# One DVE instruction of 2048 elements for two neighbouring products of a CIN kernel

## What is computed

```
e = stack(tbl_f[ids[:, f]] for f in 0..38)             # 1024 x 39 x 16, float32
xk = e
for W, b in three layers:                              # W is 39 x fields(xk) x 128
    z  = einsum('bhd,bkd,hks->bsd', e, xk, W) + b
    z  = relu(z)
    xk, direct = z[:, :64], z[:, 64:]                  # last layer: all 128 are direct
z = sum over d of the direct parts                     # 1024 x 256
y = relu(relu([z, dense_ctx] @ W_top1 + b1) @ W_top2 + b2) @ W_top3
```

## Time and profile before

| | |
|---|---|
| median of 3 runs | 1320.3 us (1320.02 to 1326.73) |
| the profiled execution | 1325.62 us, span 1323.8 us |
| granted TensorE clock, mean | 0.996 |
| instructions on DVE | 965 |
| busy share of the span | PE 94%, DVE 82%, POOL 69%, ACT 50% |
| the chain that ended last, by engine | PE 76%, POOL 10%, issue 7%, DVE 6%, ACT 1% |

### The profile page before, as it was taken

How to read it: one execution, slowest core, us unless ns; L and a number is a source line. 1 busy time by engine, 2 the same in 40 slices (tenths; PEclk the granted TensorE clock), 3 DMA queues, 4 the chain that set the end, 5 groups by cost and what they waited for, 6 DMA issues and landing times.

```text
span 1323.8 us, 15099 instructions
## 1 busy us (share of the span) xinstructions
PE 1247.7 (94%) x4078; PEld 768.8 (58%) x4078; DVE 1090.1 (82%) x965; ACT 663.1 (50%) x704; POOL 910.8 (69%) x581
## 2 busy tenths in 40 slices
PE   0289999999999999999999999999999999999989
PEld 0136666666656666666655666666666666666633
DVE  1149888989999888988998888989999888989850
ACT  1124555545554555556554555555554555555532
POOL 6668778876888678876886678886888655555520
PEclk9999999999999999999999999999999999999999
DMA  6198777787887777887897677878887777777500
GB/s 184 27 217 206 178 192 183 201 195 191 214 191 181 178 187 195 190 196 193 211 211 179 144 189 192 193 197 201 216 182 175 188 190 185 192 191 190 128 0 0
DMA packets 133859, 233.49 MB, mean 176 GB/s; under 512 B 15890, under 2 KB 23043, under 8 KB 133729
## 3 DMA queue, kind: packets, MB, share of 16 engines
q1 hardware_dynamic: 80333, 146.77, 47.5%
q10 hardware_dynamic: 43522, 83.90, 24.2%
q0 software_dynamic: 9984, 2.58, 2.2%
HBM read 229.33 MB, written 6.23 MB: 178 GB/s over the span
## 4 chain that ended last, share of the span: by engine, by line
PE 76%; POOL 10%; issue 7%; DVE 6%; ACT 1%; DMA 0%; DVEq 0%; POOLq 0%; ACTq 0%
PE z_odd L789 32%; PE z_even L789 28%; PE z_even L796 7%; POOL gathered L451 6%; POOL rest L464 5%; PE z_odd L796 4%; DVE whole L687 3%; PE whole_psum L869 2%; DVE rest L694 1%; DVE whole_psum L687 1%; PE x_even L816 1%; PE x_odd L816 1%; PE x_odd L869 1%; PE x_even L869 1%; DVE sum L718 1%
## 5 line engine op out<-in xcount | busy, mean ns | idle before, releaser
L464 POOL TENSOR_TENSOR rest<-whole,head 128x1024 fp32r<-128x1024 f32 x256 | 609.9, 2394 | 274.9 <-ACT head L559 273.8
L687 DVE TENSOR_TENSOR whole<-x_banks,x_rep 128x1024 f32<-128x1024 f32 x480 | 567.2, 1212 | 89.3 <-ACT x_banks L528 86.3
L559 ACT CAST head<-whole 128x1024 fp32r<-128x1024 f32 x256 | 268.8, 1050 | 202.9 <-DVE whole L687 139.2
L451 POOL DMA_INDIRECT gathered<-in_tbl,idx x312 | 299.0, 958 | 86.7 <-issue 77.6
L789 PE MATMUL z_odd<-whole,w_whole 128*128 128x512 f32 x468 | 219.8, 598 | 5.5 <-DVE whole L687 5.5
L559 ACT CAST head<-whole_psum 128x1024 fp32r<-128x1024 f32 x160 | 162.3, 1014 | 122.3 <-DVE whole_psum L687 115.5
L694 DVE TENSOR_TENSOR rest<-whole_psum,head 128x1024 fp32r<-128x1024 f32 x160 | 194.6, 1216 | 22.8 <-ACT head L559 22.6
L789 PE MATMUL z_odd<-head,w_rest 128*128 128x512 f32 x426 | 198.2, 465 | 6.1 <-POOL rest L464 3.4
L687 DVE TENSOR_TENSOR whole_psum<-x_banks,x_rep 128x1024 f32<-128x1024 f32 x160 | 195.9, 1224 | 8.7 <-DMA x_rep<-x_rows 7.2
L789 PE MATMUL z_even<-whole,w_whole 128*128 128x512 f32 x428 | 198.5, 592 | 0.0
L789 PE MATMUL z_even<-head,w_rest 128*128 128x512 f32 x406 | 186.1, 458 | 5.9 <-DVE rest L694 4.2
(11 more groups left out here) (74 smaller groups left out, 876.9 us busy)
## 6 DMA issues: line engine op xcount, KB each, us to landing
x_rep<-x_rows SPq DMA_DIRECT2D x160, 512.0 KB, 10.7
x_rep<-x_rows ACTq DMA_DIRECT2D x160, 512.0 KB, 11.4
x_shift<-x_rows SPq DMA_DIRECT2D x93, 546.0 KB
gathered<-in_tbl,idx POOLq DMA_INDIRECT x312
x_rows<-xt_and_ctx SPq DMA_DIRECT2D x32, 78.0 KB
x_rows<-xt_and_ctx SPq DMA_DIRECT2D x32, 40.0 KB
x_rep<-in_W_top SPq DMA_DIRECT2D x2, 512.0 KB, 12.0
w_k<-in_L_rec_w SPq DMA_DIRECT2D x1, 760.5 KB
```

The lines of the kernel that those rows point to most:

```text
L451: nc.gpsimd.indirect_dma_start(gathered[:, f, :], None, tables[f], bass.IndirectOffsetOnAxis(ap=idx[:, f:f + 1], axis=0)).then_inc(s_gathe ...
L464: nc.gpsimd.tensor_tensor(rest[:, split_slot(product)], whole_slot(product), head[:, split_slot(product)].bitcast(F32), ALU.subtract).then ...
L559: nc.scalar.copy(head[:, split_slot(product)], src).then_inc(s_head, 1)
L687: nc.vector.tensor_tensor(out[0:rows, 0:width, :], xk[0:rows, :].unsqueeze(1).to_broadcast([rows, width, N]), x0, ALU.mult).then_inc(s_pro ...
```

## The change

A product may now cover two j at once. `joined` (called for the next product not yet made) returns 2 where j is even, the next product is of kind U or P too, neither is V, and the next one's place in the ring is the next place; else 1. `product` then waits for both places, writes both with one `tensor_tensor` of 2048 elements a partition (1536 in layer 0, where the last product is the short one), and counts `s_prod` up by 2. An even j and the one after it are always in one group of `x_rep`. The calls of `rest_of` and of the reductions stay at their j, so a rest that stood between the two products comes behind the joined instruction. The numbering by places makes the joins differ from tile to tile:

| tile | layer 1 | layer 0 | layer 2 |
|---|---|---|---|
| t % 4 == 0 | U4 P5 | U2 U3 | U0 U1, P4 U5, U8 P9 |
| t % 4 == 1 | P2 P3, U4 P5 | U0 U1, U2 U3 | U0 U1, P4 U5, U8 P9 |
| t % 4 == 2 | P2 P3, U4 P5 | U0 U1, U2 U3 | P4 U5 |
| t % 4 == 3 | P2 P3, U4 P5 | U0 U1, U2 U3 | U0 U1, U8 P9 |

That is 182 joins in all. No other engine's instructions or order change.

```diff
@@ -668,7 +668,7 @@
                               ap=[list(ring[:].ap[0]), [SPC, CHUNKS0], [1, SPC], [1, FIELDS]])
             nc.vector.tensor_copy(selector.rearrange("p c (r h) -> p c r h", r=SPC), windows).then_inc(s_ring, 1)
 
-            def product(t, layer, j, xk, x0, rows):
+            def product(t, layer, j, xk, x0, rows, pairs=1):
 
                 now = t, layer, j
                 if kind_of(now) == "V":
@@ -677,16 +677,25 @@
                     if last is not None:
                         wait_rest(dve, last)
                 else:
-                    out = whole_slot(now)
-                    last = before_in_place(t, layer, j)
-                    if last is not None and kind_of(last) == "U":
-                        wait_used(dve, last)
-                    elif last is not None:
-                        wait_rest(dve, last)
+                    place = ring_place(now)
+                    out = whole[:, place:place + pairs].rearrange("p w a n -> p (w a) n")
+                    for n in range(pairs):
+                        last = before_in_place(t, layer, j + n)
+                        if last is not None and kind_of(last) == "U":
+                            wait_used(dve, last)
+                        elif last is not None:
+                            wait_rest(dve, last)
                 width = x0.shape[1]
                 nc.vector.tensor_tensor(out[0:rows, 0:width, :],
                                         xk[0:rows, :].unsqueeze(1).to_broadcast([rows, width, N]),
-                                        x0, ALU.mult).then_inc(s_prod, 1)
+                                        x0, ALU.mult).then_inc(s_prod, pairs)
+
+            def joined(t, layer, j):
+
+                kinds = KINDS[layer][j:j + 2]
+                if j % 2 or len(kinds) < 2 or "V" in kinds:
+                    return 1
+                return 2 if ring_place((t, layer, j + 1)) == ring_place((t, layer, j)) + 1 else 1
 
             def rest_of(product):
 
@@ -698,11 +707,15 @@
             def layer12(t, layer, xk, between):
 
                 later = []
+                made = 0
                 for j in range(PAIRS):
                     if layer == 1 and (2 * j) % CPL == 0:
                         wait_rep(dve, t, 2 * j // CPL)
                     c = 2 * j % CPL
-                    product(t, layer, j, xk, x_rep[:, rep_place(t, 2 * j // CPL), c:c + 2, :], P)
+                    if j == made:
+                        pairs = joined(t, layer, j)
+                        product(t, layer, j, xk, x_rep[:, rep_place(t, 2 * j // CPL), c:c + 2 * pairs, :], P, pairs)
+                        made += pairs
                     if KINDS[layer][j] == "V":
                         later.append(j)
                     if j in between:
@@ -733,10 +746,15 @@
                     nxt = t.plus(1)
                     dve.wait_ge(s_xt, nxt.count(1, 1))
                     wait(dve, s_shift, nxt.count(16 * SPC))
+                    made = 0
                     for j in range(PAIRS0):
-                        c = slice(2 * j, min(2 * j + 2, CHUNKS0))
-                        if has_layers12(t):
-                            product(t, 0, j, x0_bank[nxt.first % 2], x_shift[:, c, :], ROWS0)
+                        pairs = joined(t, 0, j) if has_layers12(t) else 1
+                        c = slice(2 * j, min(2 * j + 2 * pairs, CHUNKS0))
+                        if has_layers12(t) and j == made:
+                            product(t, 0, j, x0_bank[nxt.first % 2], x_shift[:, c, :], ROWS0, pairs)
+                            made += pairs
+                        elif has_layers12(t):
+                            continue
                         else:
                             dve.wait_ge(s_first, 1)
                             dve.wait_ge(s_select, j + 1)
```

## The result

| | before | changed |
|---|---|---|
| median | 1320.7 us (4 runs) | 1340.2 us (1336.4 to 1342.3, 4 runs) |
| changed / before | | 1.0131, 95% interval 1.0113 to 1.0149 |
| the profiled execution | 1325.6 us, span 1323.8 | 1336.4 us, span 1334.6 |
| DVE instructions, busy | 965, 1090.1 us | 783, 1080.2 us |

Slower by 1.3%, some 17 us; 0.7% was forecast, and 1335 was the upper end of the range. A second set of runs on the same edit gave 1.0130 (1.0109 to 1.0151). Ratios leave out single executions far above all others (1630 to 7246 us), which came up in the kernel before too.

A forecast was written before the change was run, and what follows sets the result against it. PE (TensorE) was taken as the bound, DVE not. Added PE waits of 6.4 + 1.9 + 0.3 + 0.6 + 0.5 = +9.7 us on the median 1320.3 gave 1330.0 us, range 1323.5 to 1335.

The forecast's parts named there:

- the waits for places: DVE, joined products waiting for both ring places: none is late, so no cost.
- the copy into emb: ScalarE copy in tile 2, behind the heads of P2 and P3: transposes touched by a few hundredths, taken as zero.
- What a join saves: DVE: 0.06 us per joint, 11 us over 182 joins, worth nothing by itself; 2.28 us for 2048 elements.
- the first rival: DVE: a joint saves its whole fixed part, 0.144 us; +6.2 us, 1326.5 us; chance 0.20.
- r6 in tile 3: DVE subtraction finishing V6, layer 2: +1.01 later, P9's 0.21 wait goes; net +0.80 in eight tiles, +6.4 us.
- the rule: PE's wait at a V or P product: end of the rest + 0.32 - end of the U before.
- r2 in tile 1: DVE subtraction finishing V2, layer 2: 1.01 later, 0.24 of new PE wait, eight times, +1.9 us.
- r2: DVE subtraction finishing V2; tile 2: 0.05 in six, 0.30 in tiles 26, 30; tile 0: nothing in six, 0.24 in 0, 28.
- the wait at P9 swallows an earlier one: PE, layer 2, tiles with gathers: P9 waits 0.25 already; a wait taken earlier is not paid again.
- Third rival: Another handover breaks (emb copy, r6 or P4): PE needs it 0.3 to 0.5 us earlier; +4 more, 1334; chance 0.10.
- That one had a mishap: Profiled execution before: a gather issued 5.71 us late, PE waited 2.85; waits therefore added to the median 1320.3.
- cover: Slack before a late handover makes PE wait: r6 in tiles 0 and 1 0.37, P4 0.4, emb copy a few hundredths.

The follow-up runs named there:

- l0_only: Changed kernel with only the 54 joins of layer 0 kept; 1.0010 of the time before.
- harmless: Changed kernel with only the 102 joins of layers 0 and 1, without P2 P3 where emb is copied; 1.0005 of the time before.
- u8_only: Changed kernel with only the 24 joins of U8 with P9 in layer 2 kept; 1.0063 of the time before.
- order_only: Kernel before, no joins, with the layer 2 DVE rests as late as the change puts them; 1.0120 of the time before.
- u0_only: Changed kernel with only the 24 joins of U0 with U1 in layer 2 kept; one execution, 148.2 us per four tiles (148.0 before).
- hoist: Changed kernel with DVE's waits for the places of U0 and U1 in layer 2 put ahead of the wait for x2; 1.0098 of the time before.
- after: The first profiled execution of the changed kernel, nothing else edited; 1336.4 us, ratio of its runs 1.0131 to the kernel before.
- again: The changed kernel run once more, no further edit; 1339.5 us, 1.0130 of the time before.
- l1_only: Changed kernel with only the 56 joins of layer 1 (P2 P3, U4 P5) kept; 1.0029 of the time before.
- p4_only: Changed kernel with only the 24 joins of P4 with U5 in layer 2 kept; one execution, 148.5 us per four tiles (148.0 before).
- half_sum: Kernel before with one layer 2 gather moved behind P9's rest and direct01's reduction halved, behind P7 and P9; 0.9965 of the time before.

## Why the prediction was wrong

The sign, the largest place and the mechanism held, and the size did not: +9.7 us was the sum, +16 us is what the stretches show, and the interval of the ratio makes 15 to 20 of it. Two terms that the sum put at nothing make the difference: the waits for places (3 to 4 us) and the copy into emb (2.5 us).

- *What a join saves*: right. 2.281 us for 2048 elements (2.28 forecast), 1.747 for 1536, 182 joins, DVE's busy time 10 us less (11 forecast), and nothing of it in the time (l0_only, harmless). Two products in a row take 2.34 us and joined 2.28, so a joint saves the 0.06, and the first rival, by which the change would have been cheaper than forecast, is out. The Trainium skill, "VectorE: DVE Perf Modes" (section on the TRN2 errata), gives (N + 151) / 0.96 ns for one instruction: the single duration agrees (2.28 against 2.29 us), but 0.157 us saved by a joint does not show between neighbours.
- *r6 in tile 3*, +1.01 and -0.21: the rule and both terms held (u8_only +0.86, order_only +0.92, as worked out for each). In the change it is +0.93, since all of layer 2 starts late.
- *The start of layer 2*, the step that failed first: "Waits for places: a joined product waits for both ... none is late." None was late, but the wait itself stands between x2 and the product, and costs 0.15 (u0_only, hoist) at the one point where DVE has been idle and PE's slack is counted from. It lies in tiles 0, 1 and 3: 0.16 more at r2 in tile 1, 0.14 at r6 in tile 3 (2.02 in place of 1.88), and 0.15 more at r2 in tile 0, where PE waits 0.39 at V2 and its wait at P9 falls from 0.23 to 0.03. That is 0.4 to 0.5 us per four tiles, 3 to 4 us in all, that the sum did not have. hoist got 0.4 back. (In u0_only, where r2 is not late, the late start shows in tile 0 at P9 instead, 0.33 for 0.23.)
- *The copy into emb*, the step that failed second: "I take zero" was 0.36, seven times, 2.5 us. Three parts of nearly equal size. First, PE needs the end of the copy 0.48 before the end of U0, not 0.32 (614.32 + 0.48 - 614.44 = 0.36; the same 0.48 to 0.50 comes out of the seven late copies of each of after, again, hoist and l1_only, and before the change 612.33 + 0.48 = 612.81 was well ahead of U0's end at 613.08). With the forecast's own times, 612.96 for the copy and 613.08 + 0.24 for U0, that alone is 0.12 of wait. I carried the 0.32 of rests over to another kind of handover. Second, the head of P2 starts 0.11 after its product (610.50 to 610.61); the trace before shows as much at P3, 609.51 to 609.62. Third, V6 waits for r2 to end, 0.12. Together 0.35. The late start adds nothing here: it moves the copy and, through the longer wait for r2, U0 as well, and in hoist the wait is 0.36 too. l1_only, where PE is not held by r2, has 0.68.
- *r2* in tile 2 and tile 0: "+0.05" and "nothing" were +0.09 and +0.20 (the latter with the late start in it). In tile 26, without gathers, 0.30 was forecast and +0.31 came; in tile 28 it was 0.24, and +0.37 came, again with the late start. That the wait at P9 swallows an earlier one held (p4_only: +0.11, +0.08 against +0.32 in tile 13).
- *Third rival*: near, with 0.10. It named the emb copy as the weakest place and priced it at most at 4 us more; it cost 2.5. The start of layer 2, which it did not name, came on top. I gave each cover as it was in one tile and did not ask what else the join moves on DVE between the two ends of that cover.
- *"That one had a mishap"*: wrong. The late gather of tile 16 is in all 17 traces, at the same instruction, the 227th gather (5.71 us before, 4.77, 4.91 and 5.05 in after, again and half_sum), and a shorter one is at the 114th in tile 5 (1.9 to 2.6 us). Most of what differs between executions of one kernel lies before tile 1: its transposes started at 130.49 before, 125.79 in the changed kernel, 129.45 in its repetition, 134.50 in order_only. In other sets the kernel before had medians of 1322.2 to 1326.4.

What stays open: why the time before tile 1 differs by up to 9 us from one execution to the next, and so what lies between the 16 us of the stretches and the 16 to 19.5 us between medians. The traces show where, and not why: from the end of the very first transposes to that of the transposes in layer 1 of tile 0, the changed kernel took 25.8 us, the kernel before 32.1 and order_only 38.2. In order_only PE stood idle 7.04 us there for one DVE product of layer 0, and its granted clock was 0.50 (1.2 GHz) from 85 to 95 us.

## What to carry to other kernels

Fewer and longer instructions help an engine that sets the pace; on one that only feeds the bound, look at what stood between the two that are joined, and at who waits for the first of them. Count the waits that an edit puts between a late release and the first instruction behind it, even if every one of them is already satisfied. Where one release starts a whole chain, a slip there reaches every handover behind it; it costs where the waiting engine is not moved by it (r2, r6), and nothing more where both sides move alike (the copy and U0). So price a cover by the difference of its two ends.

## What was not expected of the hardware

- On DVE a wait that is long satisfied, with the instructions that belong to it, costs 0.15 us when it is the third one in front of an instruction that starts from idle (x2 and two places: 1.61 us from ACT's start to DVE's; x2 and one place: 1.45; x2 alone: 1.46). The second was free.
- How early PE must be released differs by kind: a DVE or GpSimd rest must end 0.32 us before PE is free, the ACT copy read by the transposes 0.48. Whether the engine that writes or the kind of matmul that reads makes the difference, no run tells.
- A DVE instruction that has to wait for the one directly in front of it starts 1.25 us after that one (r2 to V6 in after, hoist and p4_only); without such a wait it is 1.13. At 1024 elements the dependence costs 0.12 us.
- Two executions of one program can agree to 0.05 us in each of tiles 12 to 15 and still differ by 5.1 us in the end: the changed kernel and its repetition, 3.7 of it before tile 1 and 1.4 in tile 16.
